# Stage A of a transformer block on one core: values projected through a folded convolution weight, the router as wide products with a turning, and another order of transfers at the stage's end

## The reference, cut to what matters

```python
xn = layernorm(x)                                    # x: 4 x 2048 tokens of 512
qkv = xn @ Wqkv                                      # 512 -> 3 * 512
k = compress(k, conv_w, conv_b)                      # 4 tokens -> 1, grouped by 16 heads of 32
v = compress(v, conv_w, conv_b)
out = softmax(mask(q @ k.T * 512**-0.5)) @ v @ W_out + b_out
attn = fft(fft(out, axis=-1), axis=-2).real
scores = sigmoid(xn @ router_w.T)                    # 64 experts
sb = scores + e_bias                                 # best 4 of 8 groups, then 8 experts
w = scores at the 8 experts, divided by their sum
x = x + attn + shared(xn) + sum of w * expert(xn)
```

## Time and profile before

| | us |
|---|---|
| median of 3 runs | 5562.23 (5559.91 to 5567.71) |
| the profiled execution | 5570.41 |
| its span, first to last instruction | 5568.7 |
| stage A, by PE's last product in it | 758 |

### The profile page before, as it was taken

One profiled execution on the slowest core, in us unless ns is written; L12 is line 12 of the kernel. 1 busy time (PEld: TensorE's weight loads), 2 busy tenths in 40 slices (PEclk: granted clock), 3 DMA queues, 4 the chain that ended last, 5 costly groups with the idle time before them and its releaser, 6 DMA issues. The chain is left out here.

```text
span 5568.7 us, 102394 instructions
## 1 busy us (share of the span) xinstructions
PE 5418.1 (97%) x32880; PEld 4532.0 (81%) x32880; DVE 3938.2 (71%) x8367; ACT 2584.3 (46%) x3737; POOL 2995.3 (54%) x2620
## 2 busy tenths in 40 slices
PE   8999989999999999998999999999999999999999
PEld 7888866666666666665999999999999999999886
DVE  7777767777777777776766666666666666666656
ACT  3222223333334333333666666666666666666510
POOL 2222213565555555311677777777777777777514
PEclk9999989999999999999999999999999999999999
DMA  6555554344444444443667677677787667676648
GB/s 218 180 182 182 175 158 126 113 134 120 122 130 119 138 115 122 122 129 106 126 112 158 134 144 157 134 156 165 171 210 178 134 128 164 134 155 112 159 174 283
DMA packets 475957, 832.21 MB, mean 149 GB/s; under 512 B 56212, under 2 KB 157317, under 8 KB 473102
## 3 DMA queue, kind: packets, MB, share of 16 engines
q1 hardware_dynamic: 334862, 537.99, 30.2%
q0 software_dynamic: 140928, 292.13, 28.7%
HBM read 499.48 MB, written 330.47 MB: 149 GB/s over the span
## 5 line engine op out<-in xcount | busy, mean ns | idle before, releaser
L1717 POOL DMA_INDIRECT mid_base<-e_rows,e_ox x556 | 1176.7, 2116 | 371.7 <-POOL e_ox L1712 210.2
L1828 DVE TENSOR_TENSOR e_wgu_lo<-e_wgu,e_wgu_hi 128x2048 fp32r<-128x2048 f32 x278 | 637.4, 2293 | 805.1 <-ACT e_wgu_hi L1751 633.5
L1705 POOL DMA_INDIRECT e_xg<-mid_xn,e_ix x556 | 621.3, 1118 | 338.7 <-POOL e_ix L1702 228.7
L1764 ACT CAST e_xT_hi<-e_ps_t 128x512 fp32r<-128x512 f32 x556 | 299.2, 590 | 936.6 <-PE e_ps_t L1894 936.6
L1017 POOL DMA_INDIRECT mid_ids<-b_pairs,b_cell x512 | 610.4, 1192 | 148.9 <-issue 147.9
L1907 PE MATMUL e_ps_g<-e_xT_hi,e_wgu_hi 128*128 128x256 f32 x2224 | 652.7, 293 | 1.7 <-DVE e_gated L1845 1.7
L1907 PE MATMUL e_ps_g<-e_xT_lo,e_wgu_hi 128*128 128x256 f32 x2224 | 629.7, 283 | 0.0
L1907 PE MATMUL e_ps_g<-e_xT_hi,e_wgu_lo 128*128 128x256 f32 x2224 | 629.4, 283 | 0.0
L1907 PE MATMUL e_ps_u<-e_xT_hi,e_wgu_hi 128*128 128x256 f32 x2224 | 629.4, 283 | 0.0
L1907 PE MATMUL e_ps_u<-e_xT_lo,e_wgu_hi 128*128 128x256 f32 x2224 | 629.4, 283 | 0.0
L1907 PE MATMUL e_ps_u<-e_xT_hi,e_wgu_lo 128*128 128x256 f32 x2224 | 629.4, 283 | 0.0
(11 more groups left out here) (303 smaller groups left out, 13520.4 us busy)
## 6 DMA issues: line engine op xcount, KB each, us to landing
b_xT_hi<-mid_xT_hi SPq DMA_DIRECT2D x32, 1024.0 KB
b_xT_lo<-mid_xT_lo SPq DMA_DIRECT2D x32, 1024.0 KB
mid_base<-b_x SPq DMA_DIRECT2D x32, 1024.0 KB
e_wgu<-in_gate_w SPq DMA_DIRECT2D x62, 512.0 KB
e_wgu<-in_up_w SPq DMA_DIRECT2D x62, 512.0 KB
e_wd<-in_down_w SPq DMA_DIRECT2D x62, 512.0 KB
ec_cell<-mid_base SPq DMA_DIRECT2D x88, 256.0 KB, 5.0
b_q<-mid_q_hi SPq DMA_DIRECT2D x84, 256.0 KB
```

Source lines behind the costliest of these rows:

```text
L1705: pool.indirect_dma_start(xg[s][:, i, :], None, t["xn"], bass.IndirectOffsetOnAxis(ap=ix[s][:, i:i + 1], axis=0))\
L1717: pool.indirect_dma_start(t[f"base{i}"], bass.IndirectOffsetOnAxis(ap=ox[s][:, i:i + 1], axis=0), rows[s][:, i, :], None, compute_op=ALU.a ...
L1764: act.copy(xT_hi[s][:, i * DC // 2 * RB:(i + 1) * DC // 2 * RB], ps_t[i][:, :]).then_inc(xT_hi_ready, 1)
L1828: dve.tensor_tensor(wgu_lo[s][:, :], wgu[s][:, :], wgu_hi[s][:, :].bitcast(F32), ALU.subtract)\
```

## The change

- The columns of Wqkv for v are folded with the convolution once: for each offset c, `wv[c] = Wv @ W_c`, 16 fp32 products of 512 columns in step 0 (`fold_values`), each copied to `wv_hi` by ACT and its rest to `wv_lo` by DVE. v's convolution, the `vs` tile and its copies go away. In each step v is now 48 products of 512 columns with the turned tokens as weights, in one bank (`vc`).
- For that, the tokens of a step stand in the order (p i) where it was (i p): tile i holds the tokens 4 p + i. x, `xn`, base0 and the token numbers of stage B follow; ACT writes q back in the order of tokens.
- The router takes 8 fp32r products of 512 columns, with the hi and lo parts of its weights side by side as 128 columns of weights. The two halves of the result stand on different partitions; ACT copies the bank to `halves`, which is the tile `vcs` under another name, and 4 fp32 products of 64 columns with `add_halves` (two unit matrices) add and turn them.
- The ring has 12 places in place of 16; in a step v now stands ahead of k's convolution.
- DVE does v's bias ahead of the split of the next tokens, and ACT's split waits for v's products.
- Several tiles share memory: q_hi and ks lie in `wraw`, `early`'s tiles in `wv_lo`. POOL's first splits wait for the fold.
- In step 15 constants and the clearing store come first, and q and k for B are loaded once v's products are done. The first weights of the shared expert (`raw(0)`) are loaded in B.

The diff, cut to its core:

```diff
-RING = ([("router", 0)] + [("qkv", i) for i in range(12)] + [("kc", 0), ("vc", 0), ("pos", 0)])
+RING = ([("router", 0)] + [("qk", i) for i in range(8)] + [("vc", 0), ("kc", 0), ("pos", 0)])
...
         vcs = sb("a_vcs", [P, DIM])
+        halves = vcs
...
@@ sync, step @@
                 hold(sp, xT_lo_ready, (s + 1) * DC, passed)
+                if not ahead:
+                    early.load_constants(sp, t, xn)
+                    clear(s)
...
+                if not ahead:
+                    sp.wait_ge(filled["vc"], nth("vc", s, 0))
+                    early.load(sp, t)
                 hold(sp, kc_split, s * 2 + 2, passed)
...
-                clear(s)
+                if ahead:
+                    clear(s)
@@ gpsimd @@
             inv_sqrt(0)
-            with pool.Fori(0, NSTEP - 1) as s:
+            inv_sqrt(1)
+            pool.wait_ge(fold_filled, DC * DC)
+            splits(0)
+            with pool.Fori(1, NSTEP - 1) as s:
@@ scalar, split_x and step @@
-                    act.wait_ge(filled["qkv"], nth("qkv", s - 1, 11))
+                    act.wait_ge(filled["vc"], nth("vc", s - 1, 0))
...
                 if not first:
-                    act.wait_ge(route_ready, s)
-                act.activation(sc[:, :, :].rearrange("p a e -> p (a e)"),
-                               bank[RING_BANK[("router", 0)]][:, 0:TPB * EXPERTS], ACT.Sigmoid).then_inc(emptied["router"], 1)
+                    act.wait_ge(vc_out, 16 * s)
+                act.copy(halves[:, :], bank[RING_BANK[("router", 0)]][:, :]).then_inc(emptied["router"], 1)
+                for i in range(8):
+                    if i == 2:
+                        act.wait_ge(filled["route"], nth("route", s, 0))
+                        if not first:
+                            act.wait_ge(route_ready, s)
+                        act.activation(sc[:, :, :].rearrange("p a e -> p (a e)"), bank[0][:, 0:TPB * EXPERTS], ACT.Sigmoid)\
+                            .then_inc(emptied["route"], 1)
@@ vector, step @@
                 route(s, st, first)
+                if first:
+                    for n in range(DC * DC):
...
+                        dve.wait_ge(wv_hi_ready, n + 1)
+                        dve.tensor_tensor(wv_lo[part], bank[n % 4][:, :].rearrange("p (c j) -> p c j", c=CF),
+                                          wv_hi[part].bitcast(F32), ALU.subtract).then_inc(wv_lo_ready, 1)
                 pick(s, st, first)
-                if not last:
-                    split_x(s + 1)
                 dve.wait_ge(filled["vc"], nth("vc", s, 0))
...
+                if not last:
+                    split_x(s + 1)
@@ tensor @@
+            def fold_values():
...
+                for n in range(DC * DC):
+                    k, m = n // DC, n % DC
+                    if n >= 4:
+                        pe.wait_ge(wv_lo_ready, n - 3)
+                    pe.matmul(bank[n % 4][:, :], wraw[0][:, m, k * P:(k + 1) * P], wconv[:, m, :, :].rearrange("p c n -> p (c n)"),
+                              start=True, stop=True).then_inc(fold_filled, 1)
+                pe.wait_ge(wv_lo_ready, DC * DC)
...
-                for i in range(TPB):
-                    for k in range(DC):
-                        last_i = pe.matmul(b[:, i * EXPERTS:(i + 1) * EXPERTS], xT[:, k, i * P:(i + 1) * P], wrt[:, k, :],
-                                           start=k == 0, stop=k == DC - 1)
+                pe.wait_ge(xT_lo_ready, DC * (s + 1))
+                for k in range(DC):
+                    for n, xt in enumerate((xT_hi, xT_lo)):
+                        last_i = pe.matmul(b[:, :], wrt_split[:, k, :], xt[:, k, :], start=k == 0 and n == 0,
+                                           stop=k == DC - 1 and n == 1)
...
+                    if m == 1:
+                        pe.wait_ge(emptied["router"], nth("router", s, 0))
+                        pe.wait_ge(emptied["xT"], nth("xT", s, 0))
+                        for i in range(TPB):
+                            last_i = pe.matmul(bank[0][:, i * EXPERTS:(i + 1) * EXPERTS], halves[:, i * P:(i + 1) * P],
+                                               add_halves[:, :], start=True, stop=True)
...
+                for c in range(CF):
+                    for k in range(DC):
+                        for n, (xt, wt) in enumerate(((xT_hi, wv_hi), (xT_lo, wv_hi), (xT_hi, wv_lo))):
+                            last_i = pe.matmul(b[:, :], xt[:, k, c * CPB:(c + 1) * CPB], wt[:, c, k, :],
+                                               start=c == 0 and k == 0 and n == 0, stop=c == CF - 1 and k == DC - 1 and n == 2)
@@ stage B, sync @@
-            sp.sem_inc(raw_in[0], 32)
+            load_raw(0)
```

More of the change, by code:

```diff
@@ L112, in __init__, with piece_of @@
         sb, _, sem = opener(nc, ctx, "ab_")
-        self.q = sb("q", [KN, HPC, QC], F32R)
-        self.kc = sb("kc", [KM, HPC, 2 + NC], F32R)
+        self.space = sb("space", [P, CF * DC * DIM], F32R)
+        self.ident = sb("ident", [P, P])
+        taken = 0
+        def piece_of(rows, shape):
+            nonlocal taken
+            size = int(np.prod(shape))
+            piece = self.space[0:rows, taken:taken + size]
+            taken += size
+            return piece if len(shape) == 1 else piece.rearrange("p (a n) -> p a n", a=shape[0])
+        self.q = piece_of(KN, [HPC, QC])
+        self.next_q = piece_of(KN, [HPC, QC])
+        self.kc = piece_of(KM, [HPC, 2 + NC])
+        self.null = piece_of(3 * DH, [DC * P])
+        self.null_heads = piece_of(KN, [P])
         self.vc = sb("vc", [P, NC // P, P])
-        self.null = sb("null", [3 * DH, DC * P], F32R)
-        self.null_heads = sb("null_heads", [KN, P], F32R)
         self.nullv = sb("nullv", [P, DC])
@@ L237, in stage_a @@
         w_in = sem("a_w_in")
-        wq_in = [sem(f"a_wq_in{i}") for i in range(3)]
+        wq_in = [sem(f"a_wq_in{i}") for i in range(2)]
+        wv_in = sem("a_wv_in")
+        fold_filled = sem("a_fold_filled")
+        wv_hi_ready = sem("a_wv_hi_ready")
+        wv_lo_ready = sem("a_wv_lo_ready")
         late_w_in = sem("a_late_w_in")
         wq_hi_ready = sem("a_wq_hi_ready")
+        wrt_hi_ready = sem("a_wrt_hi_ready")
+        wrt_lo_ready = sem("a_wrt_lo_ready")
         wq_lo_ready = sem("a_wq_lo_ready")
@@ L403, in step @@
                 if not first:
-                    act.wait_ge(route_ready, s)
-                act.activation(sc[:, :, :].rearrange("p a e -> p (a e)"),
-                               bank[RING_BANK[("router", 0)]][:, 0:TPB * EXPERTS], ACT.Sigmoid).then_inc(emptied["router"], 1)
[L407 to L411, removed]
+                    act.wait_ge(vc_out, 16 * s)
[7 more added lines that the diff above has]
+                            .then_inc(emptied["route"], 1)
+                    act.wait_ge(filled["qk"], nth("qk", s, i))
+                    src = bank[RING_BANK[("qk", i)]][:, :].rearrange("p (c j) -> p c j", c=CF)
                     if i == 0 and not first:
                         act.wait_ge(q_out, 32 * s)
[L414 to L419, removed]
+                    dst = qs[:, i, :].rearrange("p (j c) -> p c j", c=CF) if i < 4 else ks[:, i - 4, :, :]
+                    act.copy(dst, src).then_inc(emptied["qk"], 1)
+                if first:
+                    for n in range(DC * DC):
+                        k, m = n // DC, n % DC
+                        act.wait_ge(fold_filled, n + 1)
+                        act.copy(wv_hi[:, :, k, m * P:(m + 1) * P], bank[n % 4][:, :].rearrange("p (c j) -> p c j", c=CF))\
+                            .then_inc(wv_hi_ready, 1)
+                if not last:
+                    turned(s + 1)
                 if not last:
@@ L645, in transposes @@
                         pe.wait_ge(xn_ready, TPB * (s + 1))
+                        if not first:
+                            pe.wait_ge(emptied["route"], nth("route", s - 1, 0))
                     for i in range(TPB):
@@ L680, in step @@
                 last_i.then_inc(filled["kc"], 1)
[L681 to L687, removed]
                 b = bank_free("pos", 0, s, first)
@@ L710, in stage_b @@
         sb, ps, sem = opener(nc, ctx, "b_")
-        q = [early.q] + [sb(f"q{r}", [KN, HPC, QC], F32R) for r in range(1, 3)]
+        q = [early.q, early.next_q, sb("q2", [KN, HPC, QC], F32R)]
         kc = [early.kc, sb("kc1", [KM, HPC, 2 + NC], F32R)]
@@ L726, in stage_b @@
         att = [sb(f"att{r}", [P, QC]) for r in range(2)]
-        raw = [early.raw, sb("raw1", [P, 2 * DC * P])]
+        raw = [sb(f"raw{r}", [P, 2 * DC * P]) for r in range(2)]
         wgu_hi = sb("wgu_hi", [P, HJ, 2, DC, P], F32R)
@@ L923, in load_x @@
                     sp.wait_ge(base_out, 16 * s)
-                sp.dma_start(x[:, :, :], t["x" if s < NSTEP else "base0"][rows, :].rearrange("(i p) c -> p i c", p=P))\
+                sp.dma_start(x[:, :, :], t["x" if s < NSTEP else "base0"][rows, :].rearrange("(p i) c -> p i c", p=P))\
                     .then_inc(x_in, 16)
```

93 lines of the change are left out of this document (52 added, 41 removed).

## The result

The changed kernel is slower: 5608.1 us (median; 5603.5 to 5616.8) against 5561.1 for the kernel before on the same chip. The ratio is 1.0086, with a 95% interval of 1.0074 to 1.0098, that is 41 to 54 us more. The forecast was 5602.4, or 40 us more.

The account below looks back on a forecast made before the run. Stage A was taken to be bound by PE's own work. Later end of stage A 35, seam 3.2 and B's opening 1.9 sum to +40.2 us on the 5562.2 median: 5602.4 us, 8-in-10 range 5562 to 5626.

Parts of the forecast that it names:

- PE's work in a step: Steady step of stage A: PE's work falls from 45.95 to 41.55 us, 66 us over 15 steps without waits.
- The wait: Stage A, steps 1 to 15: PE idles 3.5 us ahead of the turning, until the vcs store lands and ACT copies.
- The clock: Behind the wait in each of 15 steps: low clock loses 2.3 us a step; chance with the wait 0.68.
- Step 0: Stage A's first step, with the fold: transposes start at 67.9, step 1's router at 84.6, 14.1 us later.
- The end of stage A: PE's end of stage A moves from 758.1 to 793.2 us, 35 us later.
- The seam: Between stages A and B: the barrier comes 3.2 us later against PE's end.
- B's opening: Start of stage B: DVE's tables come in later, 1.9 us felt in full by PE, from 0 to 3.
- The rest: The kernel behind B's opening: the same products, so given nothing.
- The clock that stays up: Rival, stage A: clock stays up through the 3.5 us wait, step 45.05 us, +5.7, 5568 us; chance 0.14.
- The store that lands earlier: Rival, stage A: vcs lands 2.8 us after issue, PE waits 1.3, -27, 5535 us; chance 0.12 including no wait.
- without a wait: Rival, stage A: PE never waits, step 41.55 us, -47, 5515 us; chance 0.12 including the earlier landing.
- DVE as the bound: Rival, stage A: DVE ends after PE, its 37.7 us loop lengthened by meeting POOL, 5630 or more; chance 0.06.

Follow-up runs that it names:

- e1: Changed kernel with the router's halves in memory of their own, so ACT's copy no longer waits for the vcs store: 5513.2 us, 44 less than the kernel before.
- e2: Changed kernel with the clearing store issued behind the store of vcs, the wait kept: 5527.2 us, 30 less than the kernel before.
- e3: Changed kernel with 14 unused products of 512 columns in PE's queue ahead of its wait, steps 1 to 15: 5574.3 us, 17 more than the kernel before.
- e9: Changed kernel unaltered, run once more on a third chip: 5550.7 us against 5502.4 for the kernel before (1.0089).
- e4: Kernel before with only the order of the tokens changed: 5558.8 us, ratio 1.0002.
- e7: Changed kernel with 7 unused products in PE's queue ahead of its wait, leaving part of it idle: 5590.6 us, 19 more than the kernel before.
- e11: e6 once more, unaltered, on the same chip as e9: 5461.0 us, ratio 0.9926 to the kernel before.
- e5: Changed kernel with the router of before, so the fold alone and no wait for the vcs store: 5534.0 us, 37 less than the kernel before.
- e6: e1 with stage B's three small tables loaded ahead of the first weights: 5521.4 us, 50 less than the kernel before.

## Why the prediction was right, point by point

*PE's work in a step.* Forecast 41.55, measured in e1, where nothing waits, 41.65. The prices from distances between starts held, that of the fold too (0.43).

*The wait.* Forecast: the turning at 11.25 us behind k's last product and a wait of 3.5. Measured 379.36 - 368.07 = 11.29, against 11.25. The idle time of 3.30 leaves out some 0.2 us of the 3.5, since the record of the last product reaches that far behind the point where the next one could start. The chain is the one put down: issue of the store 5.53 behind k (forecast 5.46), landing 5.05 (5.0). e1 takes away the shared memory and the wait goes; e2 takes away what delays the landing and the wait shrinks to 0.5.

*The clock.* The mechanism is right, the size for one step too small: 2.3 us forecast, 2.7 measured between the changed kernel and e3. Over stage A the two come closer than that, and this is in part luck. Step 1, with a wait of 2.01 us, kept the full clock, and steps 2 and 13 were at 1.2 GHz for 3.4 us in place of 6.8. From step 1's router to the end of stage A the changed kernel takes 797.0 - 86.1 = 710.9 us and e3 760.2 - 84.9 = 675.3, of which 0.95 is step 1, where the products last longer than the wait. So the clock cost some 36.6 us, where 15 x 2.3 = 34.5 was forecast. In e9, by the same reckoning, it was 33.5. The Trainium skill's rule ("TensorE: Matmul & The Clock Gate", "HAM oscillation — how this bites in real kernels"), by which each round's wait throttles PE anew, agrees with nearly all steps here: the loss came in 14 of 15, and in 13 in e9.

*Step 0.* The transposes started at 67.62, forecast 67.9, and PE's wait for the last piece of the fold was 1.40, forecast 1.6. But step 1's router came at 86.1, not 84.6: DVE was 1.44 us late with `xT_lo`, after `pick` had met POOL's split of q. As the prediction said, the wait of step 1 took it up: it was 2.01 us there instead of 3.3, and step 1 lasted 43.9. That this shorter wait would also keep the clock up the prediction did not say.

*The end of stage A.* Forecast 35 us later; the counts' last product stands at 797.0 against 757.9, that is 39.1, and in e9 it stood at 792.8. Of the 4 us between, 1.5 are step 0 and 2.1 the clock. (The terms of a step add up to 45.03, not 45.05, which is 0.3 us in all.) The seam: forecast 3.2, measured 40.0 - 39.1 = 0.9. That term was sized too large: SP launched the last three small stores (`pos`, `w8`, the counts) in 801.84 to 803.63 = 1.8 us, where it took 759.96 to 763.58 = 3.6 before. The two misses have opposite signs, so that B's start, 40.0 us later where 35 + 3.2 = 38.2 was forecast, looks better than its terms.

*B's opening.* Forecast 1.9 us. DVE had its tables 828.42 - 806.57 = 21.85 us behind B's start against 784.99 - 766.57 = 18.42, so 3.4 us later, and PE's first product of the shared expert stood 4.1 us later (13.4 against 9.3). But the whole stage was not longer: 1832.6 us against 1835.9. e4's was 1827.7, so the order of the tokens may give a few us back here.

*The rest.* "I give it nothing", with the 1.9 for B's opening, stands against the 7 us behind B's start, so a remainder of some 5 us is left, the largest miss of the sum. The changed kernel and e1 to e3 are 4 to 13 us worse by their times than by the start of B in their traces, e7 5, e9 to e11 7 to 12; e5 is level, e4 is 1 us better and e6 2. e5 and e6 have the changed kernel's order of tokens and its code of the expert stage too, so these alone don't bring it. In the profiles it stands in the expert stage, whose length runs from 2624 to 2645 us among kernels with the same code for it. What sets it was not found.

*The rivals.* The clock that stays up was put at 5568, 5.7 us above the kernel before; e3, which makes it so, is 17 above. Its step of 45.05 was right (45.1 to 45.3); what is left over is mostly the remainder above. The store that lands earlier (a wait of 1.3 us) was put at -27 and without a wait at -47; e2 with 0.5 us gave -30, e1 -44. DVE as the bound is ruled out at 41.65 us a step.

## What to carry to other kernels

When a step gets shorter, look at every buffer that takes a second tenant: the store that nobody waited for has a landing time, and the new tenant meets it as soon as the work between them shrinks. Work the landing out from its own chain (what it is issued behind, what is ahead of it in the queue) and not from its own length. And count an idle time of TensorE twice, once as the wait and once as the low clock behind it. In this loop the low clock came behind nearly every wait of 3.0 to 3.4 us, behind every second one of 1.7 and behind none of 0.5.

## What was not expected of the hardware

An idle time of 1.7 us in every step lowered the clock in every second step with great regularity (e7), while of the ten single idle times of 1.7 to 2.0 us in the kernel before, the one in the earlier trace rows among them, seven left it alone.

ACT's copy of a bank of 512 columns took 0.59 us, but 1.08 where it writes q back in the order of tokens, with a distance of four elements between writes. ACT's timeline in the changed kernel:

```profile
338.12 1.07 ACT L447 COPY a_qs<-a_bank 128x512 f32<-128x512 f32 x1 [4.30 <-PE a_bank L725]
...
343.61 0.59 ACT L447 COPY a_wraw<-a_bank 128x512 f32<-128x512 f32 x1 [1.67 <-PE a_bank L725]
```

The kernel before, which read with this distance and wrote in order, took 0.59 for all of them. ACT had room, so it cost nothing.
